# A transformer block on one NeuronCore: VectorE's base row goes to the end of its list, TensorE holds the next tile's norm flag in a register, and the weighted sum goes in front of the side products

## What is computed

```python
h = _layernorm(x) * (1 + ca) + sa
qkv = h @ Wqkv.T + bqkv             # 16 heads of 8
attn = softmax(q k^T / sqrt(8)); vals = attn @ v
x = x + ga * (vals @ Wo.T + bo)
h = _layernorm(x) * (1 + cb) + sb
probs = softmax(h @ router_w.T); topk_vals, topk_idx = top_k(probs, 2)
topk_w = topk_vals / (topk_vals.sum(-1) + 1e-06)
expert_out = einsum('nh,eho->eno', h, expert_weights)
out = ((expert_out[topk_idx] + topk_vals) * topk_w).sum(axis=0)
x = x + gb * out
```

## Time and profile before

| | |
|---|---|
| median of 3 runs | 575.02 us (574.36 to 576.14) |
| the profiled execution | 575.76 us, its span 574.0 us |
| TensorE busy | 88% of the span |
| ScalarE busy | 85% |
| VectorE busy | 65% |
| GpSimd busy | 40% |
| mean granted TensorE clock | 0.98 |

### The profile page before, as it was taken

The page is one execution under the profiler, slowest core; times in us unless marked ns, Lnnn a source line. Parts: engine busy times, 40 slices in busy tenths (PEclk is TensorE's granted clock), DMA queues, the critical chain, the costliest instruction groups (busy, mean ns, idle before and its releaser), DMA issues.

```text
span 574.0 us, 19559 instructions
## 1 busy us (share of the span) xinstructions
PE 507.4 (88%) x6667; PEld 195.9 (34%) x6667; DVE 374.4 (65%) x1258; ACT 489.5 (85%) x574; POOL 227.7 (40%) x488
## 2 busy tenths in 40 slices
PE   6879899888888988888898888899888889988987
PEld 6523233323333332333333233333323333332326
DVE  4414566667777666777766677776667777666566
ACT  1378999888889888888988888898888899888975
POOL 1101323345454334545433444543344454334444
PEclk9688999999999999999999999999999999999999
DMA  5563323333223233322323332232333222333000
GB/s 113 150 176 85 90 73 97 94 95 86 73 70 87 74 95 94 85 71 72 86 76 95 94 82 70 76 83 78 95 93 83 69 78 83 81 99 97 21 22 19
DMA packets 83342, 48.25 MB, mean 84 GB/s; under 512 B 59608, under 2 KB 74084, under 8 KB 83300
## 3 DMA queue, kind: packets, MB, share of 16 engines
q1 hardware_dynamic: 68860, 43.30, 28.0%
q10 hardware_dynamic: 14440, 4.38, 3.5%
HBM read 32.78 MB, written 14.87 MB: 83 GB/s over the span
## 4 chain that ended last, share of the span: by engine, by line
PE 61%; DVE 17%; issue 10%; ACT 7%; DMA 2%; SPq 1%; DVEq 1%; ACTq 1%; POOL 0%; POOLq 0%
PE ps_attn L819 26%; PE ps_side L724 18%; PE ps_scores L801 13%; ACT probs L608 7%; DVE bias_w L1247 5%; DVE pair_pw L1245 2%; DVE qkT L1114 2%; DVE weighted L1264 2%; DVE xhat L1100 2%; DVE qk_parts L1123 1%; PE ps_side L747 1%; DMA bo_rows<-in_L_attn_bo_dram 1%; PE ps_scores L676 1%; PE ps_scores L722 1%; DVEq L1253 1%
## 5 line engine op out<-in xcount | busy, mean ns | idle before, releaser
L608 ACT ACTIVATE probs<-ps_scores 128x1024 f32<-128x1024 f32 x512 | 479.8, 1053 | 71.7 <-PE ps_scores L801 70.6
L819 PE MATMUL ps_attn<-probs,values 128*32 128x512 f32 x2048 | 273.5, 601 | 0.1
L801 PE MATMUL ps_scores<-query_stack,key_stack 32*128 32x512 f32 x1024 | 130.6, 498 | 12.8 <-issue 8.1
L801 PEld LDWEIGHTS ps_scores<-query_stack,key_stack 32*128 32x128 f32 x1024 | 49.9, 183 | 229.9 <-ACT probs L608 198.9
L454 POOL TENSOR_SCALAR var_eps<-moments 128x1 f32<-128x1 f32 x64 | 12.3, 192 | 217.8 <-DVE moments L1191 143.0
L724 PE MATMUL ps_side<-experts_in,h2T 128*32 128x256 f32 x896 | 72.3, 390 | 4.0 <-issue 0.9
L1264 DVE TENSOR_TENSOR weighted<-ps_side,coef 128x256 f32<-128x256 f32 x114 | 47.8, 419 | 37.6 <-PE ps_side L724 36.5
L819 PEld LDWEIGHTS ps_attn<-probs,values 128*32 128x32 f32 x2048 | 57.0, 110 | 25.4 <-DVE attn L1174 8.3
L724 PE MATMUL ps_side<-ident,xhat 128*32 128x128 f32 x240 | 13.0, 289 | 38.2 <-DVE weighted L1264 37.2
L505 POOL TENSOR_TENSOR mix<-weighted 128x512 f32<-128x512 f32 x29 | 37.1, 1279 | 3.7 <-ACT weighted L626 3.7
L456 POOL TENSOR_TENSOR rstd<-var_eps,minus_half 128x1 f32<-128x1 f32 x64 | 36.2, 566 | 5.4 <-POOL var_eps L454 0.2
(11 more groups left out here) (185 smaller groups left out, 547.6 us busy)
## 6 DMA issues: line engine op xcount, KB each, us to landing
key_stack<-k_scr SPq DMA_DIRECT2D x128, 128.0 KB, 2.8
query_stack<-q_scr SPq DMA_DIRECT2D x125, 64.0 KB, 2.2
q_scr<-qk_parts SPq DMA_DIRECT2D x94, 64.0 KB, 1.7
k_scr<-qk_parts SPq DMA_DIRECT2D x64, 64.0 KB, 1.7
a_scr<-attn ACTq DMA_DIRECT2D x120, 18.0 KB
sums<-a_scr SPq DMA_DIRECT2D x31, 64.0 KB, 2.1
attnT<-a_scr SPq DMA_DIRECT2D x31, 64.0 KB, 2.2
out_dram<-out_all ACTq DMA_DIRECT2D x28, 64.0 KB, 2.7
```

What stands on the lines that cost most here:

```text
L608: nc.scalar.activation(probs[:, k % RING, g, :], ps_scores[:, slot(k, g), :], ACT.Exp, scale=SCALE)\
L801: mm = nc.tensor.matmul(out_, key_stack[p0:p0 + 32, parity, 2 * k:2 * k + 2, :].rearrange("p j r -> p (j r)"), query_stack[p0:p0 + 32, par ...
L819: mm = nc.tensor.matmul(ps_attn[q:q + 32, :], values[:, parity, g, k, :], probs[:, k % RING, g, h * HALF:(h + 1) * HALF], start=(k == 0), ...
```

## The change

Three edits. First, the base row leaves its place in front of `c_weigh` piece 0 and goes behind `c_weigh` piece 1, the end of VectorE's list for a tile; `c_x1` now waits for `base` of the same ring place, since it overwrites the x1 that `base` reads. Second, TensorE no longer loads the norm flag at a tile's start; it loads the next tile's flag behind the side product of block 5 into one of two registers. Third, in each block `weigh` stands in front of `SIDES[k]`.

```diff
@@ TensorE
+            bounded_held = [pe.alloc_register(f"bounded_held_{parity}") for parity in range(2)]
             def tile(t, parity, before, after):
...
-                k_count, q_count, bounded_count = times(pe, at[1], 64), times(pe, at[1], 64), times(pe, at[1], 1)
+                k_count, q_count, bounded_next = times(pe, at[1], 64), times(pe, at[1], 64), times(pe, at[2], 1)
...
-                reached(pe, ev["bounded_done"], bounded_count)
-                flag = pe.value_load(bounded_int[0:1, parity, :], min_val=0, max_val=1)
+                if before == 0:
+                    reached(pe, ev["bounded_done"], 1)
+                    pe.reg_load(bounded_held[0], bounded_int[0:1, 0, :])
+                flag = pe.snap(bounded_held[parity], min_val=0, max_val=1)
...
-                    SIDES[k](at, parity, before, after)
                     if k >= 2:
                         weigh(at[0], at[1], parity, k - 2)
                     elif before:
                         weigh(at[-1], at[0], 1 - parity, KT - 2 + k)
+                    SIDES[k](at, parity, before, after)
+                    if k == 5 and after:
+                        reached_apart(pe, ev["bounded_done"], bounded_next, setup_dve, SETUP_COLUMNS)
+                        pe.reg_load(bounded_held[1 - parity], bounded_int[0:1, 1 - parity, :])
@@ VectorE
             def c_x1(ps, y1, ring):
                 reached(dve, ev["attn_proj_done"], y1)
                 reached(dve, ev["x_gated_done"], y1)
+                base_before = plus(dve, y1, -2)
+                reached(dve, ev["base_done"], base_before)
...
-                if before >= 3:
-                    c_router_base(at[-3], at[-2], 1 - parity)
-
                 if before >= 3:
                     c_weigh(ps_side, at[-2], 1 - parity, 0)
                 if after == 0:
+                    c_router_base(at[-3], at[-2], 1 - parity)
...
                 if before >= 3:
                     c_weigh(ps_side, at[-2], 1 - parity, 1)
+                if before >= 3 and after:
+                    c_router_base(at[-3], at[-2], 1 - parity)
```

## The result

The changed kernel takes 584.52 us (median of 3 runs, 581.34 to 585.06) against 575.02: 1.0147 times the time of before, 95% interval 1.0086 to 1.0209. It is slower, by 1.5%. The profiled execution took 585.06 us, its span is 583.2, 9.2 more than before.

The account below looks back on a forecast made before the run. TensorE was taken to set the pace, so new waits count in full. Pair 34.12 against 33.53 gave +7.1 us in the loop, +3 outside: span 584.1, forecast 585 us, own range 581 to 591, over all 570 to 592.

Parts of the forecast that it names:

- The wait in block 6 goes: Block 6: TensorE's wait for `weighted` before the side product disappears once the base row moves, saving 1.50 us a tile.
- s: The start of block 7's side product, from which the prediction counts VectorE's later steps in us.
- The chain to `c_x1`: VectorE after block 7's side product: `base`, flag load and branch let `c_x1` start at s+3.26 (odd) or s+3.76 (even).
- The rival that the cover holds: Tile start: `c_x1` isn't late, only block 2's new wait stands against the old; pair 32.95, 571 us; chance 0.17.
- Block 2's wait: Block 2: the weighted sum waits for VectorE's copy `c_save`, a new 1.10 us in each of tiles 4 to 31.
- Block 1's side product: Block 1: waiting for `a_bounded`, it comes 3.58 (odd) or 3.68 us (even) after the tile's scores, 0.6 late.
- Between the tiles: From block 7's side product to the next tile's scores: 0.8 us, or 1.2 with the loop's jump, without TensorE's load.
- The sum: Even tile 16.91, odd 17.21, pair 34.12 against 33.53: +7.1 us in the loop, +3 outside, span 584.1.
- VectorE's idle time before `c_x1` gone: Sign expected in the profile after: no VectorE idle time before `c_x1`, while block 1's side product waits 0.5 to 0.7.
- the scores of block 1 at 1.69: Tile start: distance from the tile's first scores to those of block 1, taken over from before as 1.69 us.
- The wait for `bounded_int`: Block 1: the side product was to wait 0.5 to 0.7 us, named in the prediction as for `a_bounded`.
- the load of TensorE: Between the tiles: taking out TensorE's flag load with its checks was to remove 0.6 us; in block 5 it costs 0.

Follow-up runs that it names:

- The run with the copy first: The changed kernel with VectorE's copy of `ps_attn` (`c_save`) moved ahead of the third `weighted` and `x1hat`: 554.80 us, ratio 0.9651 to the kernel before.
- with the flag held: Kernel before with edits one and two, old order, VectorE's norm flag held in a register, loaded behind `c_save`: 536.24 us, ratio 0.9315.
- the row above: Busy times of the kernel before with edit one and VectorE's flag held in a register, old order, TensorE's own load: 539.89 us, pair 30.81.

## Why the prediction came out as it did

The forecast of 585 was met (584.5). The steps that carry its sum held, most of them to a tenth of a microsecond:

- *The wait in block 6 goes.* Scores of block 6 to those of block 7 fell from 3.45 to 1.83. The row costs 0.15, 0.16 and 0.35, as forecast; `base` starts at s+1.85 (forecast 1.89).
- *The chain to `c_x1`.* Even tile s+3.76 (3.76), odd s+3.12 (3.26). The rival that the cover holds is refuted by the rows, and by edit one alone, which would have been faster still with `x` in time (539.89 against 556.06 with VectorE's load gone).
- *Block 2's wait.* 0.96 for 1.10; 30 waits, 28.4 us in all. The sum of block 2 starts 2.03 after block 1's side product, forecast 2.10; the copy followed 0.25 after `x1hat`, where the forecast had put 0.30. The run with the copy first shows it as the cause of the loss.
- *Block 1's side product* 3.79 and 3.53 after the tile's scores (3.68 and 3.58), and from there 12.41 to block 7's (12.43).
- *Between the tiles* 1.09 and 0.71 (1.2 and 0.8).
- *The sum.* Even tile 16.91 (16.91), odd 17.02 (17.21), pair 33.93 (34.12). From tile 4 to 28 the kernel lost 4.0 us (407.4 for 403.4), not 7.1; the start lost 1.0 and the end, from tile 28, 4.2 (86.24 for 82.04), together 5.2 and not 3. The two misses nearly cancel: 9.2 in the span for 10.1. Part of the first is the sample: the average pair of before was 33.62 (403.4 over 12), a tenth longer than the one the prediction read.

Three readings were wrong, without weight in the sum. First, the prediction took 1.57 us of idle time before `c_x1` as time in which VectorE waited for the projection, and gave its rival 1.57 to spare. Its own rows say otherwise: the load ran from 256.9 to the end of the branch at 257.8 inside that time, `c_x1` could have started 0.37 later, at 258.2, and started at 258.49. The slack was some 0.3 us (with edit two alone `x` came 2.57 after block 7's side product, for 2.94). The sum used the chain and not the 1.57, so it came out; but the sign "VectorE's idle time before `c_x1` gone" did not come, since the row of `x` still shows 1.56. Second, the forecast left the scores of block 1 at 1.69 behind the tile's first. They come at 1.84 and 1.92, since they wait for ScalarE's first exponential, which now stands right behind its output store (0.76 after the scores in an even tile, 0.53 before). That lay inside the lateness of `c_x1`, so it cost nothing here; it took part of the gain when VectorE's load was removed. The wait for `bounded_int` is shorter for the same reason, 0.45 in the even tile for the 0.5 to 0.7 forecast. Third, the forecast took the load of TensorE as worth its 0.6 in each tile. It is 0.68 on average, but VectorE's chain gives nearly all of it back at block 2: 0.21 a pair.

What the experiments add is whose the loss is. Edit one is worth 20 us, edit two 7, each alone; edit three costs 53 on the kernel before and 34 where edit one is in (589.80 for 556.06). Of that the copy's wait is the greater part: TensorE's list has 28.3 us of it in that kernel, and the copy first gave 29.7 where edit two is in as well. The cause of the 2.2 us by which the start and the end differ from the estimate wasn't looked into, and why the store and not something else leads ScalarE's wait at a tile's start is read from one chain, not tested.

## What to carry to other kernels

When an order is turned round, walk every consumer of the moved result, not only the pair that is swapped: `weigh` and the side product cost the same in either order, but a copy queued behind the product's consumer cost 1 us a tile, and swapping three calls on VectorE gave it all back. Idle time that the trace puts down to another engine may be the engine's own sequencer: `x` was said to wait for TensorE while a register load and its branch ran. And before moving a slow small operation, see what makes it slow: as a reduction with one input instead of two `bias_w` fell from 1.20 to 0.16 us beside GpSimd, and that one line, in its single run, gave as much as moving the row. The reduction together with the other repairs wasn't run.

## What the runs showed of the hardware

- VectorE's load of one integer into a register takes 0.31 us, with 0.2 of register work behind it, but `x` starts 0.65 to 0.73 earlier without it (2.47 and 3.04 after block 7's side product with the flag held, 3.12 and 3.77 without). In front of `h2T` it moved that operation by 0.2 to 0.3 and the scores of block 5 by 0.27 in one tile of two; beside the copy, with 0.32 us of idle time behind it, it was free.
- A short VectorE operation with two SBUF inputs that starts while GpSimd's `mix` runs ends with it: `bias_w` within 0.02, `pair_pw` (1.00 us in place of 0.15) within 0.02, `base` 0.14 to 0.16 after. Started ahead of the second `mix` by 0.02, `bias_w` took 0.16.
- A pair of tiles came down to 30.5 us, with ScalarE busy for 30.06 and TensorE for 29.98 of a pair in the row above. From this one would expect hardly more without less work for both; no run tests it.
